# Local attention of a hybrid model: blocks of 64 queries, two heads to a matmul, values as weights, and the copies of the transposed probabilities on ScalarE

## The reference

```python
def local_attention(q, k, v):              # WINDOW = 64, 8 heads of 64
    bq = q.reshape(b, h, w, WINDOW, d) * QK_SCALE
    bk, bv = (look_around(bk), look_around(bv))      # block before + own block
    sim = jnp.einsum('bhwid,bhwjd->bhwij', bq, bk)
    mask = (i < j) | (i > j + WINDOW) | (j == -1)
    sim = jnp.where(mask, -jnp.finfo(sim.dtype).max, sim)
    attn = jax.nn.softmax(sim, axis=-1)
    return jnp.einsum('bhwij,bhwjd->bhwid', attn, bv)
def _layer(x, ...):
    h = shift_token(x)                     # half of the channels one token late
    q, k, v = split(h @ wqkv)              # l2norm, scale, rotary_xpos on q and k
    x = x + local_attention(q, k, v) @ wo
    h = layernorm(shift_token(x)) * lg + lb
    a, g = split(h @ w1 + b1)
    return x + (a * gelu(g)) @ w2 + b2
```

## Time and profile before

| | |
|---|---|
| median of 3 runs | 1996.06 us (1995.65 to 1997.3) |
| profiled execution: its time | 1996.95 us |
| its span, first to last instruction | 1995.2 us |
| PE busy | 1725.4 us (86%) |
| DVE busy | 1382.1 us (69%) |
| ACT busy | 979.5 us (49%) |
| POOL busy | 454.4 us (23%) |
| mean granted clock of TensorE | 0.928 |

### The profile page before, as it was taken

How to read it: one execution, slowest core, us unless ns; L and a number is a source line. 1 busy time by engine, 2 the same in 40 slices (tenths; PEclk the granted TensorE clock), 3 DMA queues, 4 the chain that set the end, 5 groups by cost and what they waited for, 6 DMA issues and landing times.

```text
span 1995.2 us, 33260 instructions
## 1 busy us (share of the span) xinstructions
PE 1725.4 (86%) x10812; PEld 1412.0 (71%) x10875; DVE 1382.1 (69%) x3623; ACT 979.5 (49%) x2591; POOL 454.4 (23%) x344
## 2 busy tenths in 40 slices
PE   6999989666466999999989899999968999999997
PEld 5888887334255777777777687777757777777776
DVE  4678768788956767768686565455547677687683
ACT  2354454332124565665656544434215756656654
POOL 1210010000013334334252100000013343343340
PEclk9999999676678999999999999999869999999999
DMA  4000000000010000000000000000000000000000
GB/s 143 1 1 0 0 0 1 0 1 0 0 53 1 4 3 1 3 4 3 3 1 3 2 1 0 0 0 0 0 0 3 3 1 3 3 3 4 3 1 24
DMA packets 15113, 13.87 MB, mean 7 GB/s; under 512 B 11286, under 2 KB 14138, under 8 KB 14650
## 3 DMA queue, kind: packets, MB, share of 16 engines
q1 hardware_dynamic: 15034, 12.88, 2.0%
HBM read 9.74 MB, written 1.05 MB: 5 GB/s over the span
## 4 chain that ended last, share of the span: by engine, by line
PE 50%; DVE 32%; issue 12%; ACT 5%; POOL 1%; DVEq 1%; POOLq 0%; ACTq 0%
PE bank L1653 7%; PE bank L1673 4%; PE bank L1784 4%; DVE arena_ffn L985 3%; DVE arena_attn L1000 3%; PE bank L1685 3%; DVE ssq L993 3%; PE bank L1822 3%; PE bank L1771 3%; DVE probT L725 3%; PE bank L1664 3%; DVE arena_ffn L981 3%; PE bank L1842 2%; PE bank L1826 2%; DVE nmaxF L718 2%
## 5 line engine op out<-in xcount | busy, mean ns | idle before, releaser
L556 POOL TENSOR_TENSOR arena_ffn<-arena_ffn 128x1024 f32<-128x1024 f32 x60 | 141.3, 2355 | 506.0 <-DVE arena_ffn L985 506.0
L725 DVE COPY probT<-bank 128x512 f32<-128x512 f32 x288 | 196.7, 683 | 35.5 <-PE bank L1664 35.2
L552 POOL TENSOR_TENSOR inv<-ssq,mhalf 128x16 f32<-128x16 f32 x64 | 186.3, 2911 | 76.3 <-DVE ssq L994 76.0
L1673 PE MATMUL bank<-vF,probT 128*128 128x64 f32 x1536 | 195.8, 270 | 4.9 <-DVE probT L725 2.9
L1673 PEld LDWEIGHTS bank<-vF,probT 128*128 128x128 f32 x1536 | 186.5, 192 | 11.9 <-DVE probT L725 11.6
L1653 PE MATMUL bank<-arena_setup 128*128 128x192 f32 (+1 forms) x1024 | 174.1, 304 | 7.1 <-ACT arena_setup L1419 5.5
L718 DVE TENSOR_REDUCE nmaxF<-bank 128x2 f32<-128x384 f32 (+1 forms) x192 | 114.6, 597 | 92.0 <-PE bank L1653 92.0
L1653 PEld LDWEIGHTS bank<-arena_setup 128*128 128x128 f32 x1024 | 157.1, 194 | 12.8 <-issue 1.2
L1471 ACT ACTIVATE arena_conv<-bank,nmaxF 128x192 f32<-128x192 f32 x256 | 105.6, 419 | 114.8 <-DVE nmaxF L718 111.3
L1362 ACT ACTIVATE prob<-bank,nmax 128x128 f32<-128x128 f32 (+1 forms) x256 | 90.1, 421 | 118.2 <-DVE nmax L718 90.1
L540 POOL TENSOR_TENSOR rstd<-var,mhalf 128x2 f32<-128x2 f32 x24 | 17.0, 710 | 534.2 <-DVE var L680 534.2
(11 more groups left out here) (271 smaller groups left out, 4132.3 us busy)
## 6 DMA issues: line engine op xcount, KB each, us to landing
packF<-in_packF SPq DMA_DIRECT2D x1, 3122.0 KB
arena_history<-in_packG SPq DMA_DIRECT2D x1, 2560.0 KB, 9.9
HS<-XH SPq DMA_DIRECT2D x32, 63.5 KB
X<-in_x_tiled SPq DMA_DIRECT2D x1, 1024.0 KB, 5.0
out_dram<-X SPq DMA_DIRECT2D x8, 128.0 KB, 1.9
arena_setup<-in_const_masks_a SPq DMA_DIRECT2D x1, 512.0 KB, 5.4
arena_setup<-in_const_masks_f SPq DMA_DIRECT2D x1, 512.0 KB
HS<-XH SPq DMA_DIRECT2D x32, 0.2 KB
```

The costliest lines, as they stand in the source:

```text
L552: pool.tensor_tensor(inv[:, t, :, 0], ssq[:, t, :, 0], mhalf[:, 0:16], ALU.pow).then_inc(sems["inv_ready"], 1)
L556: pool.tensor_tensor(t1[:, t], t1[:, t], t2[:, t], ALU.add).then_inc(sems["rope_sum"], 1)
L725: dve.tensor_copy(probT[:, u % 2], bank[4 + u % 2][:]).then_inc(sems["pt_copied"], 1)
L1673: ins = pe.matmul(o, probT[:, u % 2, n * P:(n + 1) * P], val, start=first, stop=(kt == keys // P - 1), skip_group_check=True)
```

## The change

Attention gets `F_UNITS = 4` units, one for each block of 64 queries, with all eight heads in each:

- Scores: the weights are the queries of two heads, zero-padded to a block diagonal (`qZ`), so one matmul gives 64 queries of both heads (128 rows) against 128 keys. The block before and the own block are picked by strided views of `kT` (`F_KEYS`). `take_qkT` pads the queries instead of the keys. The mask is 128 columns, read four times.
- `weigh` on VectorE divides the probabilities by their sums in SBUF, ahead of the transposes; `output`, `transpose_y` and the y tiles go.
- `probs_copy` on ScalarE takes the place of `attn_copy` on VectorE.
- `weigh_values`: the values of two heads are the weights and the transposed probabilities are streamed, so the result comes out transposed. `take_yT` picks the right head's rows by two copies of 64 partitions for each unit. `middle_values` builds the value rows of the third block's key range by two copies.
- All queues of `win` are written out anew. `scaled`, `transpose_qk` and `take_qkT` of the second tile of a batch move from the end of the round before into the batch's own round. `hidden_stats` moves up to second place in VectorE's queue.

```diff
-F_FROM = (0, P - F_WINDOW)
-F_UNITS = 6
+F_UNITS = T // F_WINDOW
+F_KEYS = (slice(0, 3, 2), slice(0, 3, 2), slice(1, 3), slice(1, 4, 2))
+F_MASK = (0, 1, 2, 1)
...
@@ VectorE, win
+                def weigh(u):
+                    dve.wait_ge(sems["exp_ready"], v.at("exp_ready", i, u + 1))
+                    ch.link(dve.reciprocal(rdenF[:, u], denF[:, u]))
+                    pr = prob[:, u % 2].rearrange("p (c k) -> p c k", k=P)
+                    dve.tensor_tensor(pr, pr, rdenF[:, u].broadcast_to([P, 4, P]), ALU.mult).then_inc(sems["norm_ready"], 1)
+                scaled(v, i, 1)
+                if hid:
+                    hidden_stats(*hid)
+                if nxt:
+                    rope_part(vn, ni, nl, 0, 0)
+                attn_max(v, i, 0, 4, P, nmaxF, F_SCORE_BANKS)
+                if nxt:
+                    rope_part(vn, ni, nl, 0, 1)
+                if m:
+                    gated(*m)
+                weigh(0)
...
+                if nxt:
+                    scaled(vn, ni, 0)
                 if fin:
                     final_stats(m[0], m[1])
+                local_residual(v, i, l)
+                if fin:
+                    norm_apply(m[0], m[1])
...
@@ ScalarE, win
+                if nxt:
+                    shifted(vn, ni)
+                    squares(vn, ni, 0)
                 if m:
                     prime(ACT.Gelu)
                     gelus(*m)
                     prime(ACT.Exp, 1)
+                local_exp(v, i, 0)
+                take_qkT(v, i, 1)
+                if nxt:
+                    squares(vn, ni, 1)
+                local_exp(v, i, 1)
+                probs_copy(v, i, 0)
+                local_exp(v, i, 2)
+                middle_values(v, i)
+                probs_copy(v, i, 1)
+                local_exp(v, i, 3)
                 take_yT(v, i, 0)
+                probs_copy(v, i, 2)
+                take_yT(v, i, 1)
+                probs_copy(v, i, 3)
+                take_yT(v, i, 2)
+                if hid:
+                    take_hidden(hid[0], hid[2])
+                take_yT(v, i, 3)
                 if nxt:
                     act.wait_ge(sems["pv_done"], v.at("pv_done", i, F_UNITS))
                     take_values(vn, ni)
                     take_qkT(vn, ni, 0)
...
@@ TensorE, win
+                if nxt:
+                    project_qk(vn, ni, nl, 0)
+                if m:
+                    pe.wait_ge(sems["down_used"], v.at("down_used", i, 0))
+                    hidden_gates(*m, 1)
+                local_scores(v, i, 0)
+                local_scores(v, i, 1)
+                if m:
+                    hidden_values(*m)
+                transpose_qk(v, i, 1)
+                if nxt:
+                    project_qk(vn, ni, nl, 1)
+                local_scores(v, i, 2)
+                transpose_probs(v, i, 0)
+                if m:
+                    hidden_out(*m)
+                local_scores(v, i, 3)
...
+                weigh_values(v, i, 0)
+                transpose_probs(v, i, 1)
+                transpose_probs(v, i, 2)
...
+                weigh_values(v, i, 1)
+                if nxt:
+                    project_values(vn, ni, nl, 0)
+                transpose_probs(v, i, 3)
+                weigh_values(v, i, 2)
+                weigh_values(v, i, 3)
+                if hid:
+                    pe.wait_ge(sems["yT_ready"], v.at("yT_ready", i, 3))
+                    transpose_hidden(hid[0], hid[2])
+                if nxt:
+                    project_values(vn, ni, nl, 1)
                     transpose_qk(vn, ni, 0)
+                project_out(v, i, l)
```

More of the change, by code:

```diff
@@ L1011, in win_close @@
             def win_close(v):
-                for t in range(NT):
-                    scaled(v, 0, t)
+                scaled(v, 0, 0)
             def win(n, l, i):
@@ new lines, in win @@
+                attn_max(v, i, 2, 4, P, nmaxF, F_SCORE_BANKS)
+                if nxt:
+                    rope_part(vn, ni, nl, 1, 0)
+                weigh(1)
+                attn_max(v, i, 3, 4, P, nmaxF, F_SCORE_BANKS)
+                weigh(2)
+                if m:
+                    mlp_end(m[0], m[1])
+                if nxt:
+                    rope_part(vn, ni, nl, 1, 1)
+                weigh(3)
+                if nxt:
+                    norms(vn, ni, 1, sch)
+                if hid:
+                    hidden_apply(*hid)
@@ L1438, in win_close @@
                 take_values(v, 0)
-                for t in range(NT):
-                    take_qkT(v, 0, t)
+                take_qkT(v, 0, 0)
             def gelus(v, i, l):
@@ L1700, in project_values, with project_out @@
                           start=True, stop=True).then_inc(sems["v_psum"], 1)
+            def project_out(v, i, l):
+                pe.wait_ge(sems["yT_ready"], v.at("yT_ready", i, F_UNITS))
+                for t in range(NT):
+                    for c in range(4):
+                        ins = pe.matmul(bank[6][:, t * P:(t + 1) * P], yTF[:, t, c], f_at[f"wo{l}"][:, c * C:(c + 1) * C],
+                                        start=(c == 0), stop=(c == 3))
+                ins.then_inc(sems["down_ready"], 1)
             def win_open(v, l):
@@ L1709, in win_close @@
                     project_values(v, 0, l, t)
-                for t in range(NT):
-                    transpose_qk(v, 0, t)
+                transpose_qk(v, 0, 0)
             def win(n, l, i):
@@ L2186, in constants @@
     blk = (p[:, None] // AHD == np.arange(AH)[None, :])
-    band0 = np.where((p[None, :] > p[:, None]) | (p[None, :] < p[:, None] - F_WINDOW), NEG, 0.0)
-    j = np.arange(F_FROM[1], T)
-    band1 = np.where((j[None, :] > P + p[:, None]) | (j[None, :] < P + p[:, None] - F_WINDOW), NEG, 0.0)
-    mf = np.zeros((P, 2, 512))
-    mf[:, 0] = np.tile(band0, (1, 4))
-    mf[:, 1, :2 * len(j)] = np.tile(band1, (1, 2))
+    q, k = p[:, None] % F_WINDOW, np.arange(F_WINDOW)[None, :]
+    own, back = np.where(k > q, NEG, 0.0), np.where(k < q, NEG, 0.0)
+    mf = np.stack([np.concatenate(pair, 1) for pair in ((own, np.full(own.shape, NEG)), (back, own), (own, back))], 1)
     keep = (p[:, None] <= p[None, :]) * 1.0
```

176 lines of the change are left out of this document (81 added, 95 removed).

## The result

| | before | after |
|---|---|---|
| time, median of 20 runs (us) | 1995.55 (1992.99 to 2001.63) | 2004.68 (1996.28 to 2016.09) |
| ratio | | 1.0044, 95% interval 1.003 to 1.0059 |
| profiled execution, span (us) | 1996.95, 1995.2 | 2001.32, 1999.5 |
| first local stretch, 15 intervals (us) | 456.8 | 465.1 |
| from its last residual to the next stretch's first | 420.3 | 399.8 |

The account below looks back on a forecast made before the run. VectorE was taken to bound two thirds of the old round, TensorE the rest. New rounds of 27.9 us, with closing and opening rounds, gave 1918 us; 22 for clock falls made 1940, eight in ten from 1912 to 1985.

Parts of the forecast that it names:

- the price of `weigh`: In VectorE's queue: four products, SBUF to SBUF, at 0.84 us each with reciprocal, 0.61 for the product itself.
- The landing: Shift DMAs' data for `hidden_stats` arrive 6.1 us after the residual; VectorE stands still from 1.6 to 6.1.
- VectorE's queue: The stretch of VectorE work without holes: 21.09 us before, less 8.30, plus 5.80, leaving 18.59 us a round.
- The tail: From the second `scaled` to the next residual: hand-over, second tile's transposes and output projection, 3.14 us.
- ScalarE's prices: 0.60 us per 128x512 PSUM copy; `take_yT` halves 0.38 (low end, chosen) to 0.59, four on the path.
- The copies' place: Four f32 probability copies on ScalarE; left on VectorE, 2.4 us more in its queue, 30.2 us a round, no gain.
- The clock: TensorE's clock falls in a pause before the second `project_qk`: half of 30 rounds at 1.5 us, 22 us.
- The opening rounds: Before each stretch's first residual: 2.5 us off each, or 3.5 us more with rotation starting at 4, not 7.5.
- The closing rounds: Last round of each local stretch, without rotation and squares: 24.6 us.
- The rivals: Four other cases: no clock loss (1918 or 1911), ScalarE becomes the bound (1942 or 1965), slower, nothing gained.
- Nothing gained: Rival: landing at 8.6 instead of 6.1 eats VectorE's 2.5 us; called remote; no change given 0.04.
- Slower: Rival: TensorE's clock falls twice a round, the second time in the tail; 31.8 us a round, 2037 us; chance 0.10.

Follow-up runs that it names:

- the control: The kernel before with GpSimd's rope sum cut from 1024 to 16 columns, the rest of that sum left out: 1980.19 us, ratio 0.9937.
- the fills: The changed kernel with GpSimd's rope sum cut to 16 columns and two constant fills of 1008 columns put in its place: 1938.17 us, ratio 0.9714.

## Why the prediction was wrong

**The step that failed** is the price of `weigh` in the sum of VectorE's queue: from SBUF to SBUF "the rows don't have at 512 columns", the two nearest give 0.61, "so the bounds coincide". Alone the product does take that: 0.69, or 0.61 back to back. The mean over the kernel is 1.41 us, and in the round shown the four cost 3.17 more. Put into the prediction's own sum: 27.9 + 3.2 = 31.1, and 31.03 was measured. That the sum comes out so closely is luck in part: with GpSimd's sum cut the round is 28.23, 0.3 more than 27.9, and the hold is worth 2.8 of its 3.17. Over the whole kernel the cut shows what the step missed: 2004.68 against 1934.67, 70 us.

Neither price row could have shown it. The product of `output` in the earlier trace rows, at 758.11, even runs beside a sum (757.45 to 759.81 in GpSimd's timeline) and takes its 0.69; but it reads its large operand from PSUM. And `scaled`, from SBUF, needs the sum's result, so it never meets its own. The one operation that a sum does hold in that round is the last, tiny step of `hidden_stats`. The rows of before, VectorE and GpSimd:

```profile
750.53 0.52 DVE L1084 TENSOR_SCALAR hvar<-mv 128x2 f32<-128x2 f32 x1
```

```profile
748.66 2.35 POOL L556 TENSOR_TENSOR arena_ffn<-arena_ffn 128x1024 f32<-128x1024 f32 x1 [15.62 <-DVE arena_ffn L985]
```

It takes 0.52 us and ends at 751.05, just after the sum's 751.01; in the changed kernel, away from a sum, and in the control with the sum cut, the same operation takes 0.17. That row was the warning. There was a second one: `scaled` takes 1.39 to 1.46 us instead of 1.22 in seven of its 62 instances in the kernel before, all seven beside GpSimd's copy of the next batch.

The Trainium skill ("SBUF — State Buffer", Who interferes with whom) states the rule that was missed: a VectorE instruction with two inputs from SBUF contends with a GpSimd instruction that reads SBUF, not with one that only writes it, and the later one is blocked for the whole of the first. The runs agree for the sum and for the copy, which hold the product, and for the fills, beside which it takes 0.69. They differ for GpSimd's power of 128x16, which reads SBUF too: 29 products of the changed kernel run beside it, all at 0.69, and here the measurement decides. The page also lists `tensor_scalar` among the operations that can contend when their operands meet its conditions; the 1.29 of line 993 agrees.

**The other steps.**

- *The landing*, 6.1 after the residual: the statistics start at 778.07, 6.5 after it, with 4.69 idle and the DMA as releaser. Right, 0.4 short.
- *VectorE's queue*, 18.59: from 778.07 to the end of `scaled` at 799.38 are 21.31, less the 3.17 of hold 18.14. Right but for the hold. *The tail*, 3.14: 3.21. Right.
- *ScalarE's prices*: 0.60 for the copies, 0.375 for the halves of `take_yT`. Right, and with them the choice of the low end.
- *The copies' place*: VectorE would have cost 2.4 a round by the sum; put back there, they cost 49 / 30 = 1.6. The Trainium skill ("ScalarE: Activation LUTs", Rules for kernel authors) gives plain element-wise work to VectorE (it names `relu`, `max`, `min`, `add` and `mul`, and bf16); carried over to these f32 copies out of PSUM, that would have made this kernel slower by those 1.6.
- *The clock*: half of the rounds at 1.5 us. Without the hold it fell in 13 of 30 at 29.67 - 28.23 = 1.44, and 1935 to 1938 us came out for the 1940 forecast. As a total that is luck too: the local stretches were 863 us, 11 more than 2 x 415.2 + 22, and the part between them 402 to 404, where the 420 of before less 2.5 for the opening round had been reckoned with. In the changed kernel it falls in 14 of 30, but there much of it disappears: the rounds whose second `project_qk` takes 2.67 and 2.97 us (at 813.52 and 844.54) are 31.25 and 30.91 long, about as those with 1.98 (30.66 to 31.14). Three of the 14 are 32.45 to 32.73 long.
- *The opening rounds*, 2.5 to 3.5 less: 2.1 and 3.3, each from the last add into X ahead of it (of the 2.6 above, 0.5 lie earlier). Nearly right. *The closing rounds*, 24.6: 27.21 and 28.44. Wrong; in the first, TensorE pauses 5.70 us while ScalarE waits behind the statistics, and the scores after it take 1.91 instead of 1.05. It is not the hold, since both are 28.3 to 28.4 with the sum cut; with nothing but the statistics moved back they are 22.75, so the place of the statistics costs it. How the 24.6 missed that was not traced.
- *The rivals.* None happened. "Nothing gained" comes near in time, but by a landing at 8.6, and that was 6.5. "Slower" was a second fall of the clock; slower it became by another engine's sum, which no rival had.

## What to carry to other kernels

When an edit gives VectorE an operation with all of its operands in SBUF, look up what GpSimd does at that moment: a price from a row where the two don't meet is the low end only, and for a sum or a copy on GpSimd the high end is the rest of that operation on top. A wait that the order of instructions makes (statistics asked for 4.7 us ahead of their data, a matmul queued ahead of one that is ready) can cost more than an edit saves, and when an operation is moved, every queue that waits for it must be put in the same order. Judge a change by the stretch that it touches: here 16.5 us in an untouched layer hid more than half of a loss of 28 between two profiles, and 15.7 us there swelled what putting the copies back seemed to cost, 49 us in its own stretches, to 63.

## What was not expected of the hardware

- The hold falls on products with all operands in SBUF (0.69 becomes up to 2.86) and on `TENSOR_SCALAR` steps however small (0.17 becomes 0.52, 1.30 and 1.58). The reduction over 1024 columns (line 992, in the kernel before 993) ran beside such a sum at its usual 1.21, `output`'s product from PSUM at 0.69, and the reciprocal of 128x8 at 0.19.
- GpSimd's copy of 128x256, 0.40 us with one input, holds a product as the sum does (0.87 at 793.23).
- GpSimd's power of 128x16 takes 2.91 us and reads SBUF, yet `hidden_apply` (0.31), `scaled` (1.22) and products of `weigh` (0.69) run beside it unslowed: for the first two see 797.27 and 798.16 against 797.44 above. By the rule they could have been held; why they aren't stays open.
- TensorE's clock in an untouched layer differs from profile to profile: that last batch took 42.95 us in both profiles of before, 31.1 in that of after and 30.3 in the control's. Over the 19 executions of the kernel before that are named above the mean granted clock was 0.925 to 0.938.
